# CIN tower on one core: layer 1's field pairs over 128 rows with 19 products a tile, and the top's last row one step later

## What is computed

```python
e = stack([tbl_f[ids[:, f]] for f in range(39)], axis=1)      # (1024, 39, 16)
x0 = xk = e
for W in (f0, f1, f2):                                        # (39*39,128), (128*39,128), (128*39,128)
    z = einsum('bfd,bgd->bfgd', x0, xk).reshape(b, f * g, d)
    xk = einsum('bpd,pm->bmd', z, W); outs.append(xk)
z = sum(concatenate(outs, axis=1), axis=-1)                   # (1024, 384)
h = concatenate([z, dense_ctx], axis=1)
h = maximum(h @ W_top1 + b_top1, 0)
h = maximum(h @ W_top2 + b_top2, 0)
y = h @ W_top3                                                # (1024, 1)
```

## Time and profile before

| | |
|---|---|
| median of three runs | 1300.53 us (1299.1 to 1301.32) |
| profiled execution | 1301.78 us, its span 1300.0 us |
| TensorE clock granted, mean | 0.996 |
| busy: TensorE / weight loads | 1262.0 us (97%) / 1024.4 us (79%) |
| busy: VectorE, ScalarE, GpSimd | 1050.4 (81%), 938.3 (72%), 958.0 (74%) us |
| DMA packets | 76.36 MB, mean 59 GB/s |

### The profile page before, as it was taken

How to read it: one execution, slowest core, us unless ns; L and a number is a source line. 1 busy time by engine, 2 the same in 40 slices (tenths; PEclk the granted TensorE clock), 3 DMA queues, 4 the chain that set the end, 5 groups by cost and what they waited for, 6 DMA issues and landing times. The chain is left out here.

```text
span 1300.0 us, 21778 instructions
## 1 busy us (share of the span) xinstructions
PE 1262.0 (97%) x5983; PEld 1024.4 (79%) x5983; DVE 1050.4 (81%) x3210; ACT 938.3 (72%) x3084; POOL 958.0 (74%) x743
## 2 busy tenths in 40 slices
PE   3799999999999999999999999999999999999998
PEld 2477778888788887888878888788878888788887
DVE  3498999788887888788887788968889788877873
ACT  2488788677776777677776778767777677777773
POOL 7588888678886778777886778867888678874461
PEclk9899999999999999999999999999999999999999
DMA  5573333332232333213333123333123333222000
GB/s 137 95 185 69 60 66 66 64 66 49 42 51 62 64 66 64 42 31 66 67 64 65 19 53 65 67 63 62 28 51 63 65 64 63 47 39 52 4 1 1
DMA packets 129501, 76.36 MB, mean 59 GB/s; under 512 B 90792, under 2 KB 98201, under 8 KB 129379
## 3 DMA queue, kind: packets, MB, share of 16 engines
q1 hardware_dynamic: 119139, 72.32, 27.1%
q0 software_dynamic: 10240, 2.64, 2.5%
HBM read 68.42 MB, written 3.87 MB: 56 GB/s over the span
## 5 line engine op out<-in xcount | busy, mean ns | idle before, releaser
L414 ACT ACTIVATE parts<-pieces,x_cols 128x128 f32<-128x128 f32 x2560 | 729.6, 374 | 270.1 <-PE pieces L723 219.7
L555 DVE SCALAR_TENSOR_TENSOR parts<-pieces,x_cols,parts 128x128 f32<-128x128 f32 x2432 | 685.3, 344 | 200.0 <-PE pieces L723 155.5
L721 PE MATMUL pieces<-w_hi,cur_hi 128*128 128x512 f32 (+1 forms) x1280 | 543.1, 424 | 7.3 <-issue 3.5
L723 PE MATMUL pieces<-w_hi,cur_lo 128*128 128x512 f32 (+1 forms) x1280 | 499.8, 391 | 0.0
L722 PE MATMUL pieces<-w_lo,cur_hi 128*128 128x512 f32 (+1 forms) x1280 | 499.3, 390 | 0.0
L363 POOL TENSOR_TENSOR parts<-parts 128x1024 f32<-128x1024 f32 x127 | 304.6, 2398 | 202.2 <-DVE parts L555 197.9
L354 POOL DMA_INDIRECT emb<-in_table,rows x320 | 312.3, 976 | 81.6 <-issue 66.2
L721 PEld LDWEIGHTS pieces<-w_hi,cur_hi 128*128 128x128 f32 x1280 | 241.8, 189 | 66.4 <-ACT parts L414 6.1
L722 PEld LDWEIGHTS pieces<-w_lo,cur_hi 128*128 128x128 f32 x1280 | 242.4, 189 | 50.4
L723 PEld LDWEIGHTS pieces<-w_hi,cur_lo 128*128 128x128 f32 x1280 | 241.2, 188 | 51.4
L368 POOL TENSOR_TENSOR tails<-parts 128x512 f32<-128x512 f32 x127 | 164.5, 1295 | 18.1
(11 more groups left out here) (78 smaller groups left out, 608.2 us busy)
## 6 DMA issues: line engine op xcount, KB each, us to landing
partners<-x_wide SPq DMA_DIRECT2D x62, 546.0 KB
partners<-x_wide SPq DMA_DIRECT2D x31, 468.0 KB
x_rep<-x_wide SPq DMA_DIRECT2D x96, 78.0 KB
emb<-in_table,rows POOLq DMA_INDIRECT x320
x_diag<-x_cols SPq DMA_DIRECT2D x256, 10.0 KB
x_wide<-emb SPq DMA_DIRECT2D x32, 80.0 KB
x_wide<-emb SPq DMA_DIRECT2D x32, 32.0 KB
wt<-in_wt SPq DMA_DIRECT2D x1, 1024.0 KB
```

The source lines that it names most:

```text
L414: last = nc.scalar.activation(parts[n % 2][:, 4 * i + r, :], src[:, r * H:(r + 1) * H], ACT.Copy, scale=x_cols[n // 4][:, n % 4, f:f + 1])
L555: nc.vector.scalar_tensor_tensor(acc, src[:, r * H:(r + 1) * H], x_cols[n // 4][:, n % 4, f:f + 1], acc, ALU.mult, ALU.add).then_inc(acc_d ...
L721: nc.tensor.matmul(dst[:, 0:width], hi[:, cols], w1_hi[:, ws], start=True, stop=False)
L723: nc.tensor.matmul(dst[:, 0:width], lo[:, cols], w1_hi[:, ws], start=False, stop=True).then_inc(l2d_ready if q in D_PIECES else l2a_ready, 1)
```

## The change

The 780 pairs are laid out over 128 rows. Six groups hold 18 shifts of 39 fields (117 rows) and, in the 11 rows that were free, fields 0 to 10 with shifts 18 to 23. The pairs that are still missing fit into 40 rows (fields 11 to 20 by 4 shifts), and the seventh group holds these 40 three times, 120 rows. Its pairs_hi is the rounded pair in all three sets; its pairs_lo takes the high part away in the third set alone (`take_low`, a column with -1 there and 0 elsewhere, in a SCALAR_TENSOR_TENSOR). Its weights are the high part, the low part and the high part again. So the one product of `pairs_lo` with `w0_hi` gives all three terms, and the other two are left out. Repeated pairs have a zero weight.

New beside it: `x_end`, the fields of the last group, loaded by three DMAs a tile and copied to `x_bank` by ScalarE at step 25 (`copy_x_end`), and a fourth load of `x_rep`; seven loads of `partners` instead of three; `w0` in two loads instead of five, padded to 7 x 128 rows; and VectorE waits for all of `const_loaded` before it takes w0_lo. `S_Y` becomes 159, and ScalarE's copy stays at 159.

```diff
-KPART = REP * F
-SHIFTS = F // 2 + 1
-PAIRK = (SHIFTS + REP - 1) // REP
-LAST_ROWS = (SHIFTS - REP * (PAIRK - 1)) * F
+SPARE = P - REP * F
+PAIRK = 7
+FULL = PAIRK - 1
+WHOLE_SHIFTS = REP * FULL
+END_FIELDS, END_SHIFTS = 10, 4
+END = END_FIELDS * END_SHIFTS
+LAST_ROWS = REP * END
...
+S_XEND = S_PAIR[FULL - 1] + 2
-S_Y = 158
+S_Y = 159
...
 # load_x
+                sp.dma_start(x_rep[i % 2][REP * F:P, :], first[0:SPARE, :]).then_inc(x_rep_loaded[i % 2], 16)
+                end = first[SPARE:SPARE + 1, :]
+                src = bass.AP(end.tensor, end.offset, [[0, END_SHIFTS], [COLS, END_FIELDS], [1, COLS]])
+                for r in range(REP):
+                    sp.dma_start(x_end[i % 2][r * END:(r + 1) * END, :], src).then_inc(x_end_loaded[i % 2], 16)
 # load_partners
+                    src = bass.AP(flat.tensor, flat.offset + r * COLS, [[COLS, F], [REP * COLS, FULL], [1, COLS]])
+                    sp.dma_start(partners[i % 2][r * F:(r + 1) * F, 0:FULL, :], src
+                                 ).then_inc(partners_loaded[i % 2], 16)
+                src = bass.AP(flat.tensor, flat.offset + WHOLE_SHIFTS * COLS,
+                              [[COLS, SPARE], [COLS, FULL], [1, COLS]])
+                sp.dma_start(partners[i % 2][REP * F:P, 0:FULL, :], src).then_inc(partners_loaded[i % 2], 16)
+                src = bass.AP(flat.tensor, flat.offset + (SPARE + WHOLE_SHIFTS) * COLS,
+                              [[COLS, END_SHIFTS], [COLS, END_FIELDS], [1, COLS]])
+                for r in range(REP):
+                    sp.dma_start(partners[i % 2][r * END:(r + 1) * END, FULL, :], src
+                                 ).then_inc(partners_loaded[i % 2], 16)
...
+            def copy_x_end(tile, i):
+                act.wait_ge(x_end_loaded[i % 2], (tile - i % 2) * 8 * END_LOADS + 16 * END_LOADS)
+                act.wait_ge(pairs_ready, tile * PAIRK + FULL)
+                nc.scalar.activation(x_bank[0:LAST_ROWS, :], x_end[i % 2][:], ACT.Copy).then_inc(x_bank_ready, 1)
...
-                            if at - 1 == S_Y:
+                            if at == S_Y:
                                 copy_y(u - 1)
...
+                if k < FULL:
+                    nc.vector.tensor_tensor(pairs_lo[buf][0:rows, :], src,
+                                            pairs_hi[buf][0:rows, :].bitcast(FP32), ALU.subtract
+                                            ).then_inc(pairs_lo_ready, 1)
+                else:
+                    nc.vector.scalar_tensor_tensor(pairs_lo[buf][0:rows, :], pairs_hi[buf][0:rows, :].bitcast(FP32),
+                                                   take_low[0:rows, 0:1], src, ALU.mult, ALU.add
+                                                   ).then_inc(pairs_lo_ready, 1)
...
+            dve.wait_ge(const_loaded, 3 * 16)
             dve.wait_ge(w0_hi_ready, 1)
...
-                nc.tensor.matmul(cur1_bank[:], w0_hi[0:rows, k, :], hi, start=k == 0, stop=False)
-                nc.tensor.matmul(cur1_bank[:], w0_lo[0:rows, k, :], hi, start=False, stop=False)
+                if k < FULL:
+                    nc.tensor.matmul(cur1_bank[:], w0_hi[0:rows, k, :], hi, start=k == 0, stop=False)
+                    nc.tensor.matmul(cur1_bank[:], w0_lo[0:rows, k, :], hi, start=False, stop=False)
                 nc.tensor.matmul(cur1_bank[:], w0_hi[0:rows, k, :], lo, start=False, stop=k == PAIRK - 1
                                  ).then_inc(pairs_used, 1)
```

More of the change, by code:

```diff
@@ L130, in cin_kernel @@
         x_cols = [sb(f"x_cols{i}", [P, 4, FX]) for i in range(TILES)]
[L131 to L134, removed]
+        x_rep = [sb(f"x_rep{i}", [P, COLS]) for i in range(2)]
+        x_end = [sb(f"x_end{i}", [LAST_ROWS, COLS]) for i in range(2)]
+        partners = [sb(f"partners{i}", [P, PAIRK, COLS]) for i in range(2)]
+        pairs_hi = [sb(f"pairs_hi{i}", [P, COLS], F32R) for i in range(2)]
+        pairs_lo = [sb(f"pairs_lo{i}", [P, COLS], F32R) for i in range(2)]
         cur1_hi = [sb(f"cur1_hi{i}", [P, COLS], F32R) for i in range(2)]
@@ L509, in quad @@
                             copy_x_rep(tile + 1, i + 1)
+                        if more and s == S_XEND:
+                            copy_x_end(tile + 1, i + 1)
                         if more and s in S_HIGH:
@@ L794, in _ @@
             warm_up(WARM_UP, pieces[0])
[L795 removed]
+            pe.wait_ge(const_loaded, 3 * 16)
             for k in range(PAIRK):
@@ L870 @@
     w0 = np.asarray(inputs["L0_rec_f0"])
-    rows = np.concatenate([i * F + (i + s) % F for s in range(SHIFTS)])
-    swapped = np.concatenate([(i + s) % F * F + i for s in range(1, SHIFTS)])
+    one, two = np.full((PAIRK, P), -1), np.full((PAIRK, P), -1)
+    for k in range(FULL):
+        one[k] = np.arange(P) % F
+        two[k] = one[k] + np.where(np.arange(P) < REP * F, REP * k + np.arange(P) // F, WHOLE_SHIFTS + k)
+    end = np.arange(LAST_ROWS) % END
+    one[FULL, 0:LAST_ROWS] = SPARE + end % END_FIELDS
+    two[FULL, 0:LAST_ROWS] = SPARE + WHOLE_SHIFTS + end % END_FIELDS + end // END_FIELDS
+    two %= F
+    first, swapped, seen = np.zeros((PAIRK, P, H), w0.dtype), np.zeros((PAIRK, P, H), w0.dtype), {}
+    for k in range(PAIRK):
+        for r in range(rows_of(k)):
+            a, b = one[k, r], two[k, r]
+            if seen.setdefault((min(a, b), max(a, b)), (k, r % END if k == FULL else r)) == (
+                    k, r % END if k == FULL else r):
+                first[k, r] = w0[a * F + b]
+                if a != b:
+                    swapped[k, r] = w0[b * F + a]
+    assert len(seen) == F * (F + 1) // 2
+    take_low = np.zeros((P, 2), np.float32)
+    take_low[2 * END:3 * END, 0] = -1.0
+    take_low[END:2 * END, 1] = -1.0
     field = np.minimum(np.arange(GATHERS * FIELDS), F) % F
```

86 lines of the change are left out of this document (35 added, 51 removed).

## The result

The changed kernel took 1282.14 us (median of four runs, 1281.49 to 1284.27) beside 1299.82 us for the kernel before on the same chip: ratio 0.9867, interval 0.9854 to 0.9879. Forecast were 1287.5 us and a range of 1283.0 to 1295.5. The profiled executions fell by more, from 1301.78 to 1282.42 us (spans 1300.0 to 1280.6): 19.4 us.

A forecast was written before the change was run, and what follows sets the result against it. TensorE was taken as the bound. Profiled 1301.78 - 14.5 - 2.4 + 0.4 + 0.7 - 0.4 + 3.2 = 1288.8 us, less 1.25 for the median of runs: 1287.5, range 1283 to 1295.5.

The forecast's parts named there:

- TensorE bound, 0.233 us a product: TensorE runs without gaps after the start; two products fewer per tile, 31 times, save 14.5 us.
- Rows 117 to 128 at zero: Products and VectorE forms over more rows (117 to 128, 78 to 120) take no longer: zero cost.
- The top's last row, -2.4: Quad's end: moving L783 behind piece 159 removes TensorE's 0.40 us wait for L590, six times: 2.4 us gained.
- ScalarE's copy, VectorE's new form, SyncE's eight more DMAs, at zero: Steady-state tiles: ScalarE's step 25 copy, VectorE's last pairs_lo and SyncE's added loads stay hidden, costing zero.
- Rivals 3 and 4: Every tile: waits at pieces 35 to 40 cancel the gain (1302.0, chance 0.05); step 25 copy slows it (1314.8, 0.04).
- (b): Start: weights and shift matrix grow by 0.21 MB ahead of or beside the first gathers, +0.7 us.
- (c): Start: VectorE waits for all constants, shift matrix included, before w0_lo; hidden with 1 us to spare, 0 to 1.
- (a), (d): Start: a fourth x_rep load before TensorE's first shift, +0.4 us; tile 0's last group with one product for three, -0.4.
- Stall, +3.2: Stall at 47 to 55 us ends with tile 1's transfers; 489 KB more at 151 GB/s delay it 3.2 us.
- The sign announced for it: ScalarE's restart: near 58 us if the stall hangs on bytes; near 54 or none if not.
- Rival 1: Start's stall is of timing, not bytes, and goes away: 1277.6 us, chance 0.10.
- Rival 2: Start's traffic ends by a few overloaded DMA engines, 4 x 10-row loads on four: 10.7 us for 3.2, 1295.0, chance 0.18.

The follow-up runs named there:

- e3: Kernel before with only the start's constants over 128 rows (w0 and its swap in two loads for five, shift matrix padded): ratio 0.9994.
- e12: Kernel before with tile 1's partner rows announced in three steps, a semaphore each, on chip 12: 1299.66 us, ratio 1.0003.
- e15: Same kernel as e12, run on chip 9: 1300.03 us, ratio 1.0003.
- e1: Kernel before with only the top's last row moved from step 158 to 159: 1294.08 us, ratio 0.9978.
- e2: Changed kernel with the top's last row back at step 158, ScalarE's copy at 159: 1285.83 us.
- e8: Changed kernel unaltered, run again on a chip without the extra stop: 1282.88 us, ratio 0.9895.
- e6: Changed kernel with the last group's loads as 10 x 4 rows instead of 4 x 10: 1280.63 us.
- e5: Changed kernel with 702 KB of extra, unread loads issued behind tile 1's partner rows: 1283.33 us, ratio 0.9899.
- e9: Changed kernel with tile 1's partner rows announced in three steps and its x_end loads behind them, on chip 0: 1270.23 us, ratio 0.9798.
- e14: Changed kernel unaltered, run once more on chip 9: 1281.23 us, ratio 0.9858.
- e13: Same kernel as e9, run on chip 9: 1280.72 us, ratio 0.9851.

## Why the prediction was wrong, by its own steps

- **TensorE bound, 0.233 us a product:** right. Step 34 lost 0.458 us where 0.467 was forecast.
- **Rows 117 to 128 at zero:** a term mis-sized, by 0.2 us a quad, some 1.5 us in all. The sum compared single rows at a precision of 0.01 us, too coarse for 558 products. The crumbs measured come to 0.3 us a quad, and where the 0.1 that is also in e3, e12 and e15 comes from I don't know.
- **The top's last row, -2.4:** right by mechanism, and 0.5 us too small: 0.48 us a quad by the steps of e1 and of the changed kernel where 0.40 was forecast, 2.9 us over six quads, with 2.95 us taken out of the changed kernel (e2). The sum took only the idle time that L590 ended. L806 shows no idle time for L614 or L616.
- **ScalarE's copy, VectorE's new form, SyncE's eight more DMAs, at zero:** right. 595 ns for 620, piece 26 pushed by 0.51 for 0.62 forecast, VectorE's form 742 ns where 850 was the upper estimate, and no new wait of TensorE in steady state. Rivals 3 and 4 did not come.
- **Start, (b) +0.7:** wrong in sign. The constants arrived 1.7 us earlier (21.12 to 19.40 for the first warm-up) and the first piece came 2.6 us earlier (43.3 to 40.7), where 0.7 later was forecast. I priced bytes at the backlog's 151 GB/s; what counted was 258 GB/s against 302, with more rows a load and two loads in place of five. These are two profiles; over all profiles of the two layouts (43.8 and 41.2 in the mean) it is 2.6 us too.
- **(c):** hidden, as forecast, with 0.8 us to spare for the 1 us of the sum. VectorE's timeline in the changed kernel shows the wait for the shift matrix, both halves of w1_lo, and then 0.81 us of idle time for TensorE's first bank:

```profile
18.55 0.96 DVE L647 TENSOR_TENSOR w_lo<-partners,w_hi 128x768 fp32r<-128x768 f32 x1 [9.45 <-DMA G<-in_shift_rows]
...
19.68 5.42 DVE L653 TENSOR_TENSOR w_lo<-parts,w_hi 128x2560 fp32r<-128x2560 f32 x2
25.91 0.69 DVE L594 TENSOR_TENSOR partners<-pieces,x_rep 128x512 f32<-128x512 f32 x1 [0.81 <-PE pieces L707]
```

- **(a), (d):** not seen apart.
- **Stall, +3.2:** this is the step that failed. It took the end of ScalarE's 7.73 us for "remote" for the landing of tile 1's rows, and added the new rows to it in full. It was not that wait. In the kernel before on that chip the rows were there when VectorE came to its pairs, held up by the extra stop, which the change doesn't lengthen. In the changed kernel the rows came last, but only just (0.30 us of idle time). So most of what the rows came later was spent under the extra stop: first pairs 56.01 to 56.51, only +0.5, and the start -1.0 by this pair of profiles, or +0.7 by the medians, instead of +3.4. Where no extra stop is, the rows do come later: by 3.6 us from e1 to e8, and by 5.3 from e3, which has the same early start. The 3.2 was right for the bytes and left out 2.0 us for the loads of 4 x 10 rows (e6).
- **The sign announced for it:** "a restart near 54 or none means that the stall does not hang on the bytes". It came at 55.13 with pairs at 56.51, and e5 and e9 bear the statement out: bytes that nobody waits for cost nothing that can be told, and with the same bytes the stall can be absent.
- **Rival 1 (stall goes away, 1277.6):** not here; it needed e9, and a chip without the extra stop. **Rival 2:** mechanism found (e6), price two to three times too high, and on the first chip mostly hidden like the rest.

By chips: where the extra stop is, the change gives 17.7 to 18.4 us (first pair, e14); where it isn't, 13.7 (e8), near the 13.0 forecast. Against the forecast of 13.0, the mistakes on the first chip are 4.4 us in the start and 2.0 in steady state by the profiled pair, and 2.7 and 2.0 by the medians. That e8 comes near the forecast is luck in part: by the medians its steady state gained some 2 us more than forecast, and its start took 1.5 us more back. From e1 to e8 the start took 3.8 us, close to the +3.4 of the sum (some 4.9 by the medians on e8's chip), but terms (b) and the stall erred in opposite directions and cancelled, so that closeness isn't a proof of the working. The first piece came 2.4 us earlier there (44.1 to 41.7), and the time from it to tile 1 grew by 6.2 us (38.7 to 44.9).

## What to carry to other kernels

When one engine's stop is recorded with no releaser, find what each engine behind it is waiting for in its own program order, and ask for two overlapping waits before pricing one: a change that lengthens the shorter costs nothing. A load announced by one semaphore holds its first consumer until its last row: announcing in the order of use was worth 12.7 us here, nearly as much as the whole change, though only on chips where nothing else took its place. Time both kernels on more than one chip before crediting an edit with its start: here the same pair gave 13.7 and 18.4 us.

## What the runs showed of the hardware

- **The same kernel stops for up to 10 us on some chips and not on others.** The kernel of e9 and e13 took 1270.23 us on chip 0 and 1280.72 on chip 9, and the kernel before 1296.6 and 1299.67; steady state was the same (quads of 152.6 and 152.7 us in e9 and e13). The cause is open, and each chip was used at one time only.
- **The order of a load's rows changes the busy share of the 16 DMA engines.** A tail of loads of 4 x 10 rows had a share of 0.24 to 0.29 of 16 engines and moved 75 to 86 GB/s; with the same rows as 10 x 4 it had 0.64 and 108 GB/s, and landed 2.0 us sooner. Divided by the busy engines that is some 20 GB/s each in the first tail, against 11 in the full backlog.
- **The clock is part of a stop's price.** In e8 TensorE is idle from about 48 us, and its granted clock is 0.51 (1.2 GHz) in 53 to 56 us; behind the stop its products of 512 columns start 0.43 us after one another (59.47, 59.90, 60.33 us) instead of 0.233. In e9, without the stop, it stays at 1.00 (the upper of the two levels, 2.4 GHz).
